# First cross-attention of a two-layer decoder: three units of sixteen turned by TensorE instead of two

## The reference

```python
q = _fq_sym(q, axis=-1)
k = _fq_sym(k, axis=-1)
v = _fq_sym(v, axis=2)
attn = jnp.einsum('bhqd,bhkd->bhqk', q, k)
attn = jax.nn.softmax(attn.astype(jnp.float32), axis=-1)
attn = _fq_unsigned(attn, axis=-1)
out = jnp.einsum('bhqk,bhkd->bhqd', attn, v)
out = jnp.transpose(out, (0, 2, 1, 3)).reshape(B, N, C)
return out @ Wp + bp
```

## Time and profile before

| | |
|---|---|
| median of 3 runs | 2910.21 us (2908.11 to 2911.58) |
| span of the profiled execution | 2906.6 us; the page gives no other time of it |
| PE, DVE, ACT, POOL busy over the span | 87%, 64%, 52%, 15% |
| stretch of the changed loop | 982 to 1663 us |
| DMA of the transposing queue | 507752 packets, 169.52 MB |

### The profile page before, as it was taken

The page is one execution under the profiler, slowest core; times in us unless marked ns, Lnnn a source line. Parts: engine busy times, 40 slices in busy tenths (PEclk is TensorE's granted clock), DMA queues, the critical chain, the costliest instruction groups (busy, mean ns, idle before and its releaser), DMA issues. The chain is left out here.

```text
span 2906.6 us, 47688 instructions
## 1 busy us (share of the span) xinstructions
PE 2533.4 (87%) x16768; PEld 1640.1 (56%) x16914; DVE 1860.4 (64%) x3871; ACT 1515.4 (52%) x2768; POOL 443.3 (15%) x687
## 2 busy tenths in 40 slices
PE   3999999999997567777777699799989989999998
PEld 1777777777774234444444355455556755655555
DVE  5677777777775789999999712366657732323222
ACT  1555555565563479999999611266656631111110
POOL 1112121121210212222222100011113300000000
PEclk9999999999999789999999799999999989999999
DMA  5000000000001299999999810400000011111110
GB/s 188 1 1 0 0 0 0 0 0 0 0 0 37 55 204 177 183 182 185 185 179 179 152 39 0 138 1 1 1 5 14 10 38 48 40 59 38 59 41 31
DMA packets 512491, 179.56 MB, mean 62 GB/s; under 512 B 471300, under 2 KB 499200, under 8 KB 511296
## 3 DMA queue, kind: packets, MB, share of 16 engines
q1 hardware_dynamic: 507752, 169.52, 29.4%
q10 hardware_dynamic: 4568, 7.74, 0.7%
HBM read 57.54 MB, written 2.23 MB: 21 GB/s over the span
## 5 line engine op out<-in xcount | busy, mean ns | idle before, releaser
L1640 DVE TENSOR_SCALAR_CACHE_REDUCE x_row<-x_p_s,x_nsq 128x1024 f32<-128x1024 f32 x512 | 622.1, 1278 | 28.9 <-PE x_p_s L1416 28.9
L1509 ACT ACTIVATE x_ints<-x_row,x_nb 128x2048 uint16<-128x2048 f32 x256 | 511.5, 1999 | 42.7 <-DMA x_turned<-x_ints 22.2
L1416 PE MATMUL x_p_s<-x_kT,x_qz 128*128 128x512 bf16 x929 | 296.9, 407 | 147.6 <-DVE x_row L1640 139.5
L2587 DVE TENSOR_TENSOR f_h<-f_act_g,f_p_u 128x512 f32<-128x512 f32 (+1 forms) x132 | 90.7, 687 | 506.7 <-PE f_p_y L2489 485.5
L2532 ACT ACTIVATE f_act_g<-f_p_g 128x512 f32<-128x512 f32 (+1 forms) x132 | 78.8, 597 | 550.8 <-PE f_p_g L2477 550.8
L2477 PE MATMUL f_p_g<-f_xT,f_wg 128*128 128x512 f32 x528 | 251.9, 600 | 1.2 <-ACT f_xT L2516 1.2
L2477 PE MATMUL f_p_u<-f_xT,f_wu 128*128 128x512 f32 x528 | 249.4, 595 | 0.0
L2489 PE MATMUL f_p_y<-f_wd,f_h 128*128 128x256 f32 (+1 forms) x1056 | 249.0, 379 | 0.0
L2489 PEld LDWEIGHTS f_p_y<-f_wd,f_h 128*128 128x128 f32 (+1 forms) x1056 | 200.5, 190 | 82.3 <-issue 61.4
L1416 PEld LDWEIGHTS x_p_s<-x_kT,x_qz 128*128 128x128 bf16 x1024 | 71.8, 101 | 271.0 <-DVE x_row L1640 244.9
L420 POOL TENSOR_TENSOR a_rstd<-a_ssq,neghalf 128x16 f32<-128x16 f32 x32 | 126.1, 3939 | 555.1 <-DVE a_ssq L813 555.1
(11 more groups left out here) (334 smaller groups left out, 4723.2 us busy)
## 6 DMA issues: line engine op xcount, KB each, us to landing
f_share<-f_kept SPq DMA_DIRECT2D x32, 256.0 KB, 3.1
x_turned<-x_ints SPq DMA_TRANSPOSE x224, 4.8
f_share<-f_kept SPq DMA_DIRECT2D x16, 224.0 KB, 2.9
f_share<-f_kept SPq DMA_DIRECT2D x16, 192.0 KB, 2.7
f_wg<-in_L_ffn_w_dram SPq DMA_DIRECT2D x2, 1408.0 KB, 7.9
f_wu<-in_L_ffn_w_dram SPq DMA_DIRECT2D x2, 1408.0 KB, 8.9
f_wd<-in_L_ffn_w_dram SPq DMA_DIRECT2D x1, 2816.0 KB, 13.2
f_share<-f_kept SPq DMA_DIRECT2D x16, 160.0 KB, 2.5
```

The source lines that it names most:

```text
L1416: mm = pe.matmul(p_s[n % SLOTS][:, c * BANK:(c + 1) * BANK], qz[b % 2][:, par, a, :], kT[:, a, at:at + BANK], start=True, stop=True)
L1509: act.activation(ints[k][:, :], rows[k][:, :, :].rearrange("p s n -> p (s n)"), ACT.Exp, bias=nb[:, k:k + 1], scale=-1.0, accum_out=esum[: ...
L1640: dve.tensor_scalar(rows[k][:, half, :], p_s[n % SLOTS][:, :], nsq[:, b % 2, h:h + 1], HIGHEST, ALU.mult, ALU.min, accum_out=(low if half ...
```

## The change

Unit 8 joins the units that PE turns. Its first half is a job of PE's unit 11 and its second of unit 12, after `turn_reps`; ACT copies them after its exponentials of units 10 and 11. Thus the first half waits for the bank to be free of the queries (`qz_up`) and not for the queries' projection (`q_up`), `turn_reps` waits for the four halves before it, and `turn_o` waits for the tile's last `t_read` in place of `qz_up`. ACT's copy of the turned output moves from unit 11 to 12. SP has one transfer less in each tile.

```diff
--- before.py
+++ after.py
@@ -1267,7 +1267,8 @@
     LOG_AMAX = float(np.log(AMAX))
     HIGHEST = 3.0e38
     ROWS_KEPT, SLOTS, LATE = 4, 3, 6
-    BY_ARRAY = (2, 4)
+    BY_ARRAY = (2, 4, 8)
+    BEFORE_REPS = 4
     TURNS = 2 * len(BY_ARRAY)
     PER_TILE = 2 * PAIRS
     UNITS = B * PER_TILE
@@ -1379,7 +1380,7 @@
             def turn_reps(b):
                 pe.wait_ge(q_up, b + 1)
                 pe.wait_ge(rep_up, b + 1)
-                after(pe, t_read, TURNS * b)
+                after(pe, t_read, TURNS * (b - 1) + BEFORE_REPS)
                 for a in range(PAIRS):
                     mm = pe.transpose(p_w[:, :].bitcast(BF16)[:, a * P:(a + 1) * P],
                                       qrep[:, 2 * a:2 * a + 2, :, :].rearrange("p a c d -> p (a c d)"), core.identb[:, :])
@@ -1387,7 +1388,7 @@
 
             def turn_o(b):
                 pe.wait_ge(o_up, b + 1)
-                pe.wait_ge(qz_up, min(B, b + 3))
+                pe.wait_ge(t_read, TURNS * min(B, b + 2))
                 after(pe, y_up, b)
                 for t in range(KT):
                     mm = pe.transpose(p_w[:, t * P:(t + 1) * P], o[:, t * P:(t + 1) * P], core.ident[:, :])
@@ -1424,7 +1425,9 @@
                         pe.wait_ge(t_read, turns(u) + half)
                     if not half:
                         pe.wait_ge(e_up, u + 1)
-                        if b + 1 < B:
+                        if b + 1 < B and turns(u) % TURNS >= BEFORE_REPS:
+                            pe.wait_ge(qz_up, b + 2)
+                        elif b + 1 < B:
                             pe.wait_ge(q_up, b + 2)
                         else:
                             pe.wait_ge(y_up, b - 1)
@@ -1461,7 +1464,7 @@
                     values(u - LATE)
                 jobs(u, {1: [(turn_x, 1)], 3: [(project_q, 1)], 5: [(turn_ints(2, 0), 0)], 6: [(turn_ints(2, 1), 0)],
                          7: [(turn_ints(4, 0), 0)], 8: [(turn_ints(4, 1), 0)],
-                         10: [(turn_reps, 1)], 13: [(turn_o, -1)], 15: [(project_o, -1)]})
+                         10: [(turn_reps, 1)], 11: [(turn_ints(8, 0), 0)], 12: [(turn_ints(8, 1), 0)], 13: [(turn_o, -1)], 15: [(project_o, -1)]})
 
         @block.scalar
         def _(act):
@@ -1527,7 +1530,8 @@
                 if u < UNITS:
                     exps(u)
                 jobs(u, {1: [(query_up, 1)], 4: [(ints_up(2, 0), 0)], 5: [(ints_up(2, 1), 0)], 6: [(ints_up(4, 0), 0)], 7: [(ints_up(4, 1), 0)],
-                         8: [(reps_up(0), 1)], 9: [(reps_up(1), 1)], 11: [(o_turned_up, -1)], 14: [(result_up, -1)]})
+                         8: [(reps_up(0), 1)], 9: [(reps_up(1), 1)],
+                         10: [(ints_up(8, 0), 0)], 11: [(ints_up(8, 1), 0)], 12: [(o_turned_up, -1)], 14: [(result_up, -1)]})
 
         @block.gpsimd
         def _(pool):
```

## The result

The changed kernel takes 2920.7 us (median of 13 runs) against 2908.7 for the kernel before: ratio 1.0045, 95% interval 1.0034 to 1.0055. It is slower by 12 to 13 us; 2927.2 was forecast.

The account below looks back on a forecast made before the run. The prediction took the first cross-attention's attend loop as bound by DVE, ACT 7% behind. Wait 14.6 us plus clock 2.4, transfers and copies at nothing, made 17.0 us: 2923.6 in a profile, 2927.2 as median, range 2908 to 2941.

Parts of the forecast that it names:

- The wait: PE stands 2.2 us for qz_up in unit 11; DVE stalls 0.79 and 0.18 us, 14.6 us over 15 tiles.
- The clock at the wait: PE's standing at unit 11 leaves about 1.3 us busy, so the clock falls as the turn begins, adding 0.83 us.
- The clock before project_o: Turns and scores crowd in ahead of project_o, so the clock fall there and its 0.82 us stall should go.
- The trade: A clock fall at the wait replaces the one before project_o, even in ten tiles or so.
- the whole term: Net clock effect of falls at the wait and stalls gone before project_o: plus 2.4 us, bounds minus 11.4 to plus 12.5.
- The transfers: Sixteen fewer transposing transfers, one per tile, counted at nothing; at most some 2.5 us off the tile 1 stall.
- The first rival: No trade: clock falls at the wait and still before project_o, 27 us, 2937; chance 0.22.
- The second: Absorbed: the new stall replaces the old 0.76 us in each of 15 tiles, leaving 3.2 us, 2913; chance 0.16.
- The third: Transfers set the stage's pace, so fewer of them give about -17 us, 2893; chance 0.09.

Follow-up runs that it names:

- the turns that nobody needs: Kernel before, plus sixteen transposes a tile in PE's units 12 and 13 behind qz_up, of data nobody reads, no copy added or transfer removed; ratio 0.9993.
- the wait alone: Kernel before, with only a wait for qz_up added in PE's unit 11, nothing turned there, no copy added, no transfer removed; ratio 1.0010.
- the transfer put back: Changed kernel (unit 8 by PE), plus a same-size transposing transfer into a spare buffer nobody reads, 224 transfers again; ratio 1.0051.
- the copies side by side: Changed kernel, with ACT emptying the bank of the queries in both copies after unit 8, later copies moved one unit earlier; 2903.4 us, ratio 0.9990.

## Why the prediction was right

**The wait.** Its steps held to 0.03 us in a late tile: 0.78 and 0.15 against 0.79 and 0.18, and nothing at turn_o. Summed over the timeline of the first profile after, the passes of unit 12 waited 17.3 us and those of unit 13 3.3, together 20.6. At full clock alone it would have been about the 14.6 of the forecast. With PE's standing cut from 34.2 to 6.1 us and all the work kept, the whole loss went (loop 658.2), so this is shown, not argued.

**The clock at the wait.** Expected: a fall in nearly every tile, 0.83 us each, 12.5 at most. Seven of fifteen tiles had a first stall of 1.39 us or more, and 7 x 0.83 = 5.8 us is nearly all of the 6.0 that lie between 14.6 and 20.6. The step that failed is the one from PE busy some 1.3 us to a fall in nearly every tile: in the stretch from 1486.4 it was busy 1.13 us and none followed. Why the clock fell in tile 7 and not in tile 11 stays open.

**The clock before project_o.** The trade came as forecast: no tile after has the 0.82 us stall. Its size was off. The forecast took ten such stalls, about 8 us; the first profile of before had eight, the other two three and five. The mean of the three profiles has 7.1 us of stalls outside tile 1, after has 0.2 beside units 12 and 13: 6.9 us given back, against 6.0 that the falls at the wait cost. So the whole term came to about minus 1 where plus 2.4 was taken. That it was near is partly luck: up to 12.5 was put down for falls at the wait and 6.0 came, some 8 to be given back and 6.9 were, and that from stalls of which some were not TensorE's (below). Beside the first profile alone the late tiles lost nothing: they take 40.87 us each, 81.7 a pair, where that one had 81.92. Most late tiles of the kernel before's other two profiles take 39.76.

The Trainium skill's rule that transposes do not count as activity of the array the way matmuls do (TensorE: Matmul & The Clock Gate, Part 4: PE-mode transpose) was taken to keep these stalls. They went, but that does not refute it. Sixteen transposes and nothing else added left none of them (the turns that nobody needs; the three profiles of before have 8, 3 and 5), and so did the wait alone, with no transpose added. A nearer look speaks against the rule without deciding it. The windows view of an earlier tile of the changed kernel, around its wait:

```profile
1365.00:1368.40 3.40, 1.31 (x13) 0.92 (x15) 2.62 (x5) 3.35 (x4) 0.57 (x2) 1.00 0.43 84
1368.40:1371.80 3.40, 2.36 (x45) 1.70 (x43) 3.24 (x5) 3.38 (x6) 0.29 (x1) 1.00 0.89 170
```

And the timeline of the turn in it:

```profile
1367.04 0.61 PE L1436 MATMUL x_p_w<-identb,x_ints 128*128 128x128 bf16 x8 [2.27 <-ACT x_qz L1489]
```

Of 1.31 us of PE 0.61 are transposes, and the clock stayed at 1.00. With the wait alone PE was busy 0.99 us at the same place, none of it transposes, and the clock fell to 0.50. Without its transposes the first has less PE work (0.70 us) than the second, and yet it did not fall. These are two chosen stretches, not a test.

**The transfers.** Counted at nothing, with 2.5 us as the most in tile 1. Tile 1's stall fell from 10.5 us (mean of three, its small neighbour of 0.5 included) to 8.9: 1.5 us. The missing transfer does not explain it: with the transfer put back it was 8.9 as well, and with 208 transfers and the copies side by side it was 9.8. What fits is that the new stall makes tile 0 longer, 47.33 us for 45.64, so that DVE comes 1.7 us later to the place where it waits in tile 1, and waits that much less. That is read from these numbers and not tested.

That no DVE wait but tile 1's follows a transfer was a misreading. The timeline of the kernel before, in its tile 3:

```profile
1134.10 2.00 ACT L1509 ACTIVATE x_ints<-x_row,x_nb 128x2048 uint16<-128x2048 f32 x1 [1.96 <-DMA x_turned<-x_ints]
1136.10 0.56 ACT L1517 COPY x_turned<-x_p_w 128x512 int32<-128x512 int32 x1
1136.72 0.45 PEld L1433 LDWEIGHTS x_p_w<-identb,x_ints 128*128 128x128 bf16 x8 [2.12 <-ACT x_turned L1517]
1138.16 1.28 DVE L1640 TENSOR_SCALAR_CACHE_REDUCE x_row<-x_p_s,x_nsq 128x1024 f32<-128x1024 f32 x1 [1.31 <-PE x_p_s L1416]
```

The wait of DVE is put down to PE, whose wait is put down to ACT, and only ACT's is put down to the transfer. Tiles 2 to 4 have three DVE waits of this kind, 2.3 us, in the 11.4 us that the forecast gave to TensorE. In the changed kernel this chain costs nearly nothing (0.2 us of small stalls outside tile 1).

**The sum.** 20.6 - 6.9 - 1.5 = 12.2 us of DVE idle time, against 13.0 in the loop and 12 to 13 in the medians; forecast 17.0. The first rival (2937) did not come, as the trade was made. The second (2913) had it right that the old stalls go. It was too low because it had nothing for the falls at the wait (6.0 us) and took the old stalls at 11.4 us, where the mean of three profiles has 7.1. The third, transfers as the pace, fell: at 208 transfers the changed loop was slower, and at 240 the loop, 663.5 us, lay within the three of before (657.9 to 665.0).

## What to carry to other kernels

A bank that one engine fills and another empties is a chain of its own: before a job is put behind another on the same bank, count what the emptying engine does between the two (here two copies with a 2 us exponential between them), and compare it with the time to the next job (2.4 us). The same work one unit later, or with the two copies side by side, was no slower than the kernel before. A wait is put down to the engine just ahead; before a sum of waits is given to that engine, follow a few of them back to where the chain begins. And take more than one profile of a kernel whose stalls hang on the clock, before its stalls are used as a term.

## What the runs showed of the hardware

The same program's loop took 665.0, 657.9 and 658.0 us in three profiles, with 11, 6 and 5 us of short stalls outside tile 1 and the same instructions; the changed one took 673.4 and 673.1. PE standing for 2.3 us for the bank was followed by half clock in seven of fifteen tiles, seen in a first stall of 1.39 us or more, in an eighth a little later (0.99 us at unit 13), and in the others not. Half clock made eight weight loads of a turn 0.77 us where they are 0.45. A transposing transfer of 512 KB within SBUF landed 4.2 to 7.0 us after its issue, median 4.6 to 4.8, in every version, from 208 to 240 of them in the loop; only in the first two tiles, where the next stage's weights are loaded from the same queue, one took 11.2 to 13.6 us.
